# GpSimd's and ScalarE's block loops written out, indices taken straight from the slot tables

## What is computed

```python
logits = x @ router_w + router_b
probs = jax.nn.softmax(logits, axis=-1)
top_v, top_i = jax.lax.top_k(probs, TOP_K)          # TOP_K = 2 of 8 experts
...
gate = jnp.einsum('td,edi->eti', x, gate_w) + gate_b[:, None, :]
up = jnp.einsum('td,edi->eti', x, up_w) + up_b[:, None, :]
h = jax.nn.silu(gate) * up
expert_out = jnp.einsum('eti,eid->etd', h, down_w) + down_b[:, None, :]
y = jnp.einsum('te,etd->td', weights, expert_out)
...
t = t + y
```

## Time and profile before

| | us |
|---|---|
| median of 3 runs | 454.5 (454.16 to 454.62) |
| span of the profiled execution | 453.7 |
| TensorE busy in the span | 346.5 |
| VectorE busy | 343.3 |
| GpSimd busy | 288.8 |
| ScalarE busy | 209.2 |
| first `down` (block 0) starts at | 252.14 |
| `down` of block 36 starts at | 432.27 |

### The profile page before, as it was taken

How to read it: one execution, slowest core, us unless ns; L and a number is a source line. 1 busy time by engine, 2 the same in 40 slices (tenths; PEclk the granted TensorE clock), 3 DMA queues, 4 the chain that set the end, 5 groups by cost and what they waited for, 6 DMA issues and landing times.

```text
span 453.7 us, 13159 instructions
## 1 busy us (share of the span) xinstructions
PE 346.5 (76%) x4491; PEld 214.4 (47%) x4492; DVE 343.3 (76%) x693; ACT 209.2 (46%) x343; POOL 288.8 (64%) x459
## 2 busy tenths in 40 slices
PE   0078677767866766697259998999999999999971
PEld 0077434444444454542023654656566566565540
DVE  6988799799899999877882776666776776677650
ACT  1047637755956857645501433334434434433430
POOL 5616456666666666644585367777877878788651
PEclk9997568668668668689569999999999999999995
DMA  8410002322322222507764132333233333323322
GB/s 197 123 36 1 2 2 96 95 94 97 95 92 92 92 95 94 144 2 194 219 248 139 25 48 46 48 56 58 46 56 55 51 49 55 58 46 58 56 25 23
DMA packets 24960, 35.27 MB, mean 78 GB/s; under 512 B 4992, under 2 KB 18304, under 8 KB 24160
## 3 DMA queue, kind: packets, MB, share of 16 engines
q1 hardware_dynamic: 16256, 24.46, 17.5%
q0 software_dynamic: 7488, 10.23, 14.1%
q10 hardware_dynamic: 1184, 0.14, 0.2%
HBM read 25.39 MB, written 9.44 MB: 77 GB/s over the span
## 4 chain that ended last, share of the span: by engine, by line
PE 25%; DVE 23%; issue 19%; POOL 13%; DMA 9%; ACT 5%; DVEq 2%; POOLq 1%; SPq 1%; ACTq 0%
PE bank L881 6%; DMA w_stage<-token_rows,q_hi 5%; POOL w_stage L513 4%; PE bank L902 3%; POOL small L509 3%; DVE att L1348 2%; PE bank L549 2%; DVE s_exp L1314 2%; DVE v_exp L1367 2%; PE bank L777 2%; DVE q_exp L1382 2%; POOL v_exp L488 2%; PE bank L664 2%; DVE maxes L1307 2%; DMA token_rows<-z_stack 1%
## 5 line engine op out<-in xcount | busy, mean ns | idle before, releaser
L881 PE MATMUL bank<-w_exp,w_stage 128*128 x468 | 113.7, 380 | 1.3 <-issue 0.2
L526 POOL DMA_INDIRECT out_dram<-w_stage,q_hi x39 | 62.4, 1600 | 16.9 <-issue 16.9
L881 PEld LDWEIGHTS bank<-w_exp,w_stage 128*128 128x128 f16 x468 | 45.6, 97 | 41.8 <-issue 4.6
L408 POOL TENSOR_TENSOR w_exp<-w_stage,w_exp 128x1024 f16<-128x1024 f32 (+1 forms) x24 | 51.0, 2129 | 22.4 <-ACT w_exp L1041 22.4
L902 PE MATMUL bank<-w_exp,q_exp 128*128 x468 | 58.6, 276 | 2.1 <-DVE q_exp L1587 2.1
L513 POOL DMA_INDIRECT w_stage<-token_rows,q_hi x39 | 48.1, 1234 | 6.0 <-issue 6.0
L1570 DVE TENSOR_TENSOR v_exp<-bank,x_rows 128x512 f32<-128x512 f32 x39 | 27.0, 692 | 32.9 <-PE bank L881 32.8
L1146 ACT ACTIVATE w_stage<-w_stage,gate 128x256 f32<-128x256 f32 x39 | 19.8, 508 | 68.2 <-DVE w_stage L1592 68.2
L902 PEld LDWEIGHTS bank<-w_exp,q_exp 128*128 128x128 f16 x468 | 43.0, 98 | 11.8 <-issue 5.4
L1127 ACT ACTIVATE w_stage<-bank 128x256 f16<-128x256 f32 x39 | 14.9, 383 | 52.9 <-PE bank L869 52.9
L1587 DVE TENSOR_TENSOR q_exp<-bank,q_exp 128x512 f16<-128x512 f32 x39 | 27.0, 692 | 10.2 <-ACT q_exp L1138 10.0
(11 more groups left out here) (253 smaller groups left out, 814.2 us busy)
## 6 DMA issues: line engine op xcount, KB each, us to landing
w_stage<-in_L_ffn_gate_w_dram SPq DMA_DIRECT2D x8, 512.0 KB, 3.5
w_stage<-in_L_ffn_up_w_dram SPq DMA_DIRECT2D x8, 512.0 KB, 3.5
w_stage<-in_L_ffn_down_w_dram SPq DMA_DIRECT2D x8, 512.0 KB, 3.5
x_rows<-in_x_dram SPq DMA_DIRECT2D x8, 256.0 KB, 6.1
out_dram<-x_rows SPq DMA_DIRECT2D x4, 512.0 KB, 6.0
token_rows<-z_stack SPq DMA_DIRECT2D x4, 512.0 KB, 6.0
x_rows<-in_L_ffn_gate_b_dram SPq DMA_DIRECT2D x1, 2048.0 KB, 11.6
z_stack<-in_L_ffn_up_b_dram SPq DMA_DIRECT2D x2, 1024.0 KB, 6.8
```

What stands on the lines that cost most here:

```text
L408: pool.tensor_tensor(lo, w_stage[:, k, :], hi, ALU.subtract).then_inc(s["w_lo_done"], 1)
L526: pool.indirect_dma_start(out, bass.IndirectOffsetOnAxis(s_idx[par], 0), yw[par], None, compute_op=ALU.add).then_inc(s["y_scattered"], 16)
L881: mm = pe.matmul(GU[par][k][:], xs[par][:, c, :], w_exp[:, w * W_EXP + k * W_PIECE + c * FF:][:, bass.ds(e, FF)], start=(n == 0), stop=(n ...
```

## The change

On GpSimd the loop is written out in Python, so that each block's number is a constant. The index copies and the four one-word multiplies go; the indirect DMAs take their column straight from `t_gather` and `t_scatter`, and the semaphore waits stand on the DMAs themselves. The wait for the gather's own buffer (`x_got`) and those for the copies (`gcol_ready`, `scol_ready`) go too. On ScalarE the loop is written out, and `weigh` of block b waits for the landing of the scatter of b-2 by `y_scattered`. VectorE's and TensorE's programs are not changed.

```diff
-            def gather(turn, par, first=False):
-
-                b = 2 * turn + par
-                if not first:
+            def gather(b):
+
+                if b >= 2:
                     pool.wait_ge(s["xt_ps"], b - 1)
-                    pool.wait_ge(s[f"x_got{par}"], 16 * turn)
-                    pool.wait_ge(s["gcol_ready"], b)
-                    pool.tensor_tensor(hold[0], one_word, one_word, ALU.mult)
-                pool.tensor_copy(g_idx[par], t_gather[:, bass.ds(b, 1)]).then_inc(s["gcol_ready"], 1)
-                pool.wait_ge(s["gcol_ready"], b + 1)
-                pool.tensor_tensor(hold[1], one_word, one_word, ALU.mult)
-                pool.indirect_dma_start(xg[par], None, token_rows, bass.IndirectOffsetOnAxis(g_idx[par], 0))\
-                    .then_inc(s[f"x_got{par}"], 16)
-
-            def scatter(b, par, first=False):
-
-                if not first:
+                pool.indirect_dma_start(xg[b % 2], None, token_rows,
+                                        bass.IndirectOffsetOnAxis(t_gather[:, b:b + 1], 0))\
+                    .then_inc(s[f"x_got{b % 2}"], 16)
+
+            def scatter(b):
+
+                if b >= 1:
                     pool.wait_ge(s["y_scattered"], 16 * b)
-                    pool.wait_ge(s["scol_ready"], b)
-                    pool.tensor_tensor(hold[2], one_word, one_word, ALU.mult)
-                pool.tensor_copy(s_idx[par], t_scatter[:, bass.ds(b, 1)]).then_inc(s["scol_ready"], 1)
-                pool.wait_ge(s["scol_ready"], b + 1)
                 pool.wait_ge(s["y_ready"], b + 1)
-                pool.tensor_tensor(hold[3], one_word, one_word, ALU.mult)
-                pool.indirect_dma_start(out, bass.IndirectOffsetOnAxis(s_idx[par], 0), yw[par], None,
+                pool.indirect_dma_start(out, bass.IndirectOffsetOnAxis(t_scatter[:, b:b + 1], 0), yw[b % 2], None,
                                         compute_op=ALU.add).then_inc(s["y_scattered"], 16)
 
-            gather(0, 0, first=True)
-            gather(0, 1, first=True)
-            gather(1, 0)
-            gather(1, 1)
-            scatter(0, 0, first=True)
-            with pool.Fori(0, 2 * BODY - 1) as i:
-                gather(i + 2, 0)
-                scatter(2 * i + 1, 1)
-                gather(i + 2, 1)
-                scatter(2 * i + 2, 0)
-            gather(2 * BODY + 1, 0)
-            for b in range(4 * BODY - 1, BLOCKS):
-                scatter(b, b % 2)
+            gather(0)
+            gather(1)
+            for b in range(BLOCKS):
+                if b + 2 < BLOCKS:
+                    gather(b + 2)
+                scatter(b)
...
@@ -1141,8 +1119,8 @@
...
-                if not first:
-                    act.wait_ge(s["scol_ready"], b)
+                if b >= 2:
+                    act.wait_ge(s["y_scattered"], 16 * (b - 1))
...
-            with act.Fori(0, BODY) as i:
-                for k in range(4):
-                    act_block(4 * i + k + 1, (k + 1) % 2)
+            for b in range(1, BLOCKS - 2):
+                act_block(b, b % 2)
```

More of the change, by code:

```diff
@@ L215, in build @@
         r_tab = k_lo[:].bitcast(fp32)
-        g_idx = [r_ints[:, 128 + i:129 + i] for i in range(2)]
-        s_idx = [r_ints[:, 130 + i:131 + i] for i in range(2)]
         ga_flat = gate[:].rearrange("p a b -> p (a b)")
@@ L245, in build @@
             block_ready values_pool place_ready tab_ps tables_ready bias_rows up_rows zero_ready pad_out
-            gcol_ready scol_ready x_got0 x_got1 xt_ps xh_ready xl_ready gu_ps gadd_ready silu_ready uadd_ready
+            x_got0 x_got1 xt_ps xh_ready xl_ready gu_ps gadd_ready silu_ready uadd_ready
             h_ready ht_ps hh_ready hl_ready y_ps yadd_ready y_ready y_scattered""".split()
@@ L496, in _ @@
             pool.wait_ge(s["pad_out"], 16)
-            hold, one_word = [small[0:1, 152 + i:153 + i] for i in range(4)], t_weight[0:1, 0:1]
-            def gather(turn, par, first=False):
-                b = 2 * turn + par
-                if not first:
+            def gather(b):
+                if b >= 2:
                     pool.wait_ge(s["xt_ps"], b - 1)
-                    pool.wait_ge(s[f"x_got{par}"], 16 * turn)
-                    pool.wait_ge(s["gcol_ready"], b)
-                    pool.tensor_tensor(hold[0], one_word, one_word, ALU.mult)
-                pool.tensor_copy(g_idx[par], t_gather[:, bass.ds(b, 1)]).then_inc(s["gcol_ready"], 1)
-                pool.wait_ge(s["gcol_ready"], b + 1)
-                pool.tensor_tensor(hold[1], one_word, one_word, ALU.mult)
-                pool.indirect_dma_start(xg[par], None, token_rows, bass.IndirectOffsetOnAxis(g_idx[par], 0))\
-                    .then_inc(s[f"x_got{par}"], 16)
```

## The result

The changed kernel takes **610.4 us** (median of 4 runs, 608.3 to 611.6) against 454.6 us for the kernel before; the ratio is 1.343 (1.339 to 1.347). The forecast was 607 us, its range 566 to 645. The profiled execution is the fastest of the four; its span is 606.5 us.

A forecast was written before the change was run, and what follows sets the result against it. The gather-scatter ring, not TensorE's own work, was taken as the bound. Paid every block, 1.70 + 3.20 + 0.13 + 3.06 + 0.35 = 8.44, plus 0.8 for the clock, 9.24 us over 35 rounds: 607 us, range 566 to 645.

The forecast's parts named there:

- The order: GpSimd's scatter of b is followed by the gather of b+3, not b+4: the round is paid every block, not every two.
- the same ring: Way from scatter through gather, tokens, `down` and weighing to a scatter: 10.07 us before, paid once for two blocks.
- the scatters' own chain: Each scatter on GpSimd waits for the one before, 3.8 us after its start: over long before `y_ready` in 8 us rounds.
- The length of a round: Scatter to scatter in the changed kernel: 8.44 us a block at full clock, 9.24 us with the low clock.
- scatter to gather: GpSimd, from scatter's start to gather's start: 1.70 us (1.60 to 1.75), where it was 2.27 before.
- weighing's end to scatter: From ScalarE's weighing to GpSimd's scatter start: 0.35 us (0.15 to 0.84), where it was 0.84 with the multiply.
- the rival of the queued transfer: Gather's transfer queues behind the scatter's: round of 10.24 us, 643 us in all; chance 0.16, shared with upper ends.
- The ends: Tokens of block 3 start at 260.11, those of block 38 at 583.5; the tail after them adds 1.0 us.
- The clock: TensorE's rests ahead of tokens and `down` lower its clock: 1.0 us in 8 rounds of 10, 0.8 us a round.
- the rival in which it stays up: TensorE keeps full clock: round of 8.44 us, 578 us in all; chance 0.15.
- ScalarE's new wait: Weighing of b waits for the landing of the scatter of b−2, 3.8 us after its start: nothing waits there.
- The faster rival: Gathers are not held, TensorE's 4.55 us a block sets the pace: 16 us less, 438 us; chance 0.04.

## Why the prediction was right

**The order** was the step that carried it, and it holds in both directions: done alone it costs 191 us, undone it gives back 163. That the trace of before already held the same ring, at two blocks a round, is confirmed by the kernel before with one gather more ahead: the waits for gathers vanish and TensorE's pace goes from 5.00 to 4.80 us. The whole kernel gained only 1.8 us by it, because a second bound lay close behind, the scatters' own chain of 4.9 us a block, which the prediction had called harmless in the new order, rightly, and had not priced in the old one.

**The length of a round** was put at 9.24 us and measured at 9.22; the tokens of block 3 were to start at 260.11 and started at 260.08. That is better than the terms deserve. The measured ones here are means of the 36 rounds from the scatter of block 0 to that of block 36, (587.84 − 255.23) / 36 = 9.24 us each:

| term, us | taken | measured |
|---|---|---|
| scatter to gather | 1.70 | 1.89 |
| gather to landing | 3.20 | 2.97 |
| landing to tokens | 0.13 | 0.13 |
| tokens to weighing's end, full clock | 3.06 | 2.86 |
| weighing's end to scatter | 0.35 | 0.80 |
| low clock, mean | 0.80 | 0.59 (3.45 − 2.86) |

Two terms were too small, by 0.64 us together, and three too large, by 0.64 together. That they cancel is luck; the path was right, its pieces were known to a few tenths.

Between scatter and gather there is an issue gap of 0.30 us behind a scatter, not the 0.15 seen behind a multiply, so the gathers start 1.89 us after the scatter, beyond the 1.8 named as a sign. The landing was shorter than the median of 3.2 before (median 2.8, the mean above it by some rounds of 3.5 to 3.8). Its closeness to the scatter's transfer did not lengthen it: in the kernel before with the changed order the gather starts 2.27 us behind the scatter and takes 2.9. So the rival of the queued transfer falls; why most gathers took longer before is not settled. The clearest miss is the way from the weighing to the scatter. I had taken it that the 0.84 us of before was in good part the multiply; it is the start of the indirect DMA after its wait, and removing the multiply saved 0.04 us.

The ends have their own two errors that cancel: the tokens of block 38 start at 582.68, 0.8 us earlier than said, and from there to the end the kernel takes 2.1 us more than before, not 1.0. So the span came to 606.5, said 606.2. The median stands 3.9 us above that span, not 0.8, and that is most of the difference between 607 and 610.4.

**The clock**: that it falls in the rests and is low over `down` in many rounds was right, and the rival in which it stays up (578 us) falls. 25 low rounds of 36 are near the share of 8 in 10, but in most of them the clock is low only for a part of the way, so that the mean is 0.59 us by the rounds and 0.49 by the test with the clock kept up. A wholly low `down` is dearer than I said: 407.38 to 411.69 from the tokens to the weighing's end is 4.31 us against 2.87, since `down` takes 2.77 there; the 2.46 that I had used began in a microsecond with a mean granted clock of 0.70. The Trainium skill, page "TensorE: Matmul & The Clock Gate", section "HAM oscillation — how this bites in real kernels", describes a kernel in which every turn starts at half clock. This trace agrees only in part: 11 of 36 rounds kept the full clock over `down`, as the 8.53 us round beside the 9.82 one shows.

**ScalarE's new wait** cost nothing, as said. Its loop was put at nothing and was worth 0.10 us a round: the weighing starts 0.04 us after the bias instead of 0.14, and that is half of the 0.20 between 3.06 and 2.86. **The rule on branches** (the Trainium skill, page "Runtime: NRT & Kernel Launch", section "Instruction fetch mechanics") is that a taken branch can force a fetch. TensorE's loop agrees, with 5.02 us at its turn and 4.73 elsewhere, though no run shows that a fetch is what the 0.29 us are. ScalarE's does not: its 0.10 us lay in every block and not at the turn. The loops of GpSimd and ScalarE gained 1.8 and 1.4 us of 454 when written out alone, which is little against the order.

**The faster rival** falls for the order of the change, and its time was wrong for the old order too. With gathers not held, TensorE's pace is 4.80 us, not 4.55, and the kernel 447.8 us, not 438. I had taken the pace from two starts in the chain of waits, and a piece of that chain begins only where the piece before it ends. In the timeline of before the same two `down` groups start 4.71 us apart (368.08 − 363.37), and the turn of TensorE's loop is not among them:

```profile
363.37 1.47 PE L902 MATMUL bank<-w_exp,q_exp 128*128 x12
...
368.08 1.48 PE L902 MATMUL bank<-w_exp,q_exp 128*128 x12
```

The same reading had made the ring look like 0.45 us of loss in each block; only about 0.2 us of it was. The 5.9 us of waits in the earlier trace rows, 0.16 a block, had said so.

## What to carry to other kernels

When a loop is written out or rewritten, count how many transfers are issued ahead of the first consumer before and after: an engine that runs in order holds every prefetch that stands behind a wait, and one buffer's lead less turned a ring paid every second block into one paid every block, 163 us of 610. Look for the ring in the old trace first; the sum of its parts gave the new time to a per cent here, but with luck, since single parts were off by up to 0.45 us in 9.24. With the lead restored the other edits are worth 1.4% on the kernel before; with TensorE's loop written out too it is 1.6% (446.2 us).

## What was not expected of the hardware

An indirect DMA on GpSimd starts 0.80 us after ScalarE's result for it is ready, whether its wait stands on the DMA or, at 0.84 us, on a multiply ahead of it. With rests of 3.3 us in the mean the granted clock was low over `down` in 25 rounds and full in 11; filling them with useless matmuls gained 18.6 us of 610. And a multiply that adds 0.04 us to the round moved the kernel by 12.7 us, of which at most 3.4 were left with the clock kept up, so small differences between kernels with such rests say little about the edit.
